# Two attention stages and the feed-forwards behind them: the first two norms of each feed-forward placed among the attention's last slots

## The reference

```python
def _mha(x, y, ..., causal):
    xn, yn = _ln(x, lnx_g, lnx_b), _ln(y, lny_g, lny_b)
    q, k, v = ...                                  # 16 heads of 32
    a = softmax(einsum('bhsd,bhtd->bhst', q, k) * D ** (-0.5))
    if causal: a = a * mask
    o = einsum('bhst,bhtd->bhsd', a, v)
    x_out = x + o @ li1_w + li1_b
    h = gelu(_ln(x_out, ln3_g, ln3_b) @ li2_w + li2_b)
    return x_out + h @ li3_w + li3_b
x = _ln(xx, ln1_g, ln1_b)
x = x + _mha(x, x, a1_..., causal=True)            # self attention, second feed-forward
x = _ln(x, ln2_g, ln2_b)
return x + _mha(x, ee, a2_..., causal=False)       # cross attention, third feed-forward
```

## Time and profile before

| what | before |
|---|---|
| median of 3 runs | 1454.49 us (1454.26 to 1460.39) |
| the profiled execution, its own time | 1445.23 us |
| its span | 1443.5 us |
| TensorE busy | 1334.6 us |
| VectorE busy | 988.5 us |
| ScalarE busy | 845.6 us |
| GpSimd busy | 653.1 us |
| first feed-forward norm behind self attention starts | 965.32 us |
| the same behind cross attention | 1234.29 us |

### The profile page before, as it was taken

How to read it: one execution, slowest core, us unless ns; L and a number is a source line. 1 busy time by engine, 2 the same in 40 slices (tenths; PEclk the granted TensorE clock), 3 DMA queues, 4 the chain that set the end, 5 groups by cost and what they waited for, 6 DMA issues and landing times.

```text
span 1443.5 us, 42854 instructions
## 1 busy us (share of the span) xinstructions
PE 1334.6 (92%) x17894; PEld 872.2 (60%) x17912; DVE 988.5 (68%) x2236; ACT 845.6 (59%) x1325; POOL 653.1 (45%) x1118
## 2 busy tenths in 40 slices
PE   6899999997999999989999999888989999899996
PEld 3455555554455554466677677656767777677685
DVE  5688887875555555578888988645577887676233
ACT  3577777775666566577677677543466666432231
POOL 4455555543001003246666665333347775455255
PEclk7899999998999999999999999999999999999898
DMA  7000000000600000000000000002011111032451
GB/s 222 3 3 3 3 3 3 3 3 2 161 8 0 1 1 1 1 2 32 17 32 21 29 32 21 28 31 60 1 32 46 47 47 46 30 92 85 129 156 52
DMA packets 55186, 53.78 MB, mean 37 GB/s; under 512 B 9305, under 2 KB 49245, under 8 KB 54738
## 3 DMA queue, kind: packets, MB, share of 16 engines
q1 hardware_dynamic: 51154, 44.24, 10.0%
q0 software_dynamic: 2816, 6.11, 1.2%
q10 hardware_dynamic: 1024, 0.69, 0.2%
HBM read 20.34 MB, written 14.49 MB: 24 GB/s over the span
## 4 chain that ended last, share of the span: by engine, by line
PE 64%; DVE 14%; POOL 6%; DMA 5%; issue 4%; SPq 4%; ACT 3%; ACTq 0%; POOLq 0%; DVEq 0%
PE psum L1538 5%; PE psum L941 4%; PE psum L942 4%; PE psum L943 4%; PE psum L1215 4%; PE psum L1566 3%; PE psum L1179 3%; PE psum L2572 3%; PE psum L2547 3%; SPq L795 2%; DVE b_nm L1621 2%; DMA a_QT<-a_nmT 2%; DVE a_nm L603 2%; PE psum L521 2%; DVE c_nm L2069 2%
## 5 line engine op out<-in xcount | busy, mean ns | idle before, releaser
L1621 DVE TENSOR_REDUCE b_nm<-psum 128x4 f16<-128x1024 f32 x128 | 157.2, 1228 | 45.1 <-PE psum L1543 45.0
L720 ACT ACTIVATE a_prob<-psum 128x768 f32<-128x768 f32 (+1 forms) x160 | 136.1, 853 | 63.1 <-PE psum L458 61.4
L603 DVE TENSOR_REDUCE a_nm<-psum 128x4 f16<-128x1024 f32 (+1 forms) x96 | 117.2, 1222 | 42.4 <-PE psum L488 29.0
L772 POOL TENSOR_SCALAR_AFFINE_SELECT a_prob<-a_prob 128x512 f32<-128x512 f32 x128 | 82.1, 641 | 125.5 <-ACT a_prob L720 125.3
L171 POOL TENSOR_TENSOR f_ln_rstd<-f_ln_tmp,pow_half 128x4 f32<-128x4 f32 x24 | 25.4, 1058 | 203.0 <-DVE f_ln_tmp L160 202.9
L1069 ACT ACTIVATE xo_sb<-psum,f_w_h_s 128x512 f32<-128x512 f32 x64 | 44.0, 688 | 85.6 <-PE psum L943 85.6
L1538 PE MATMUL psum<-b_QTh,b_KTh 32*128 32x256 f16 x512 | 70.7, 272 | 16.2 <-DVE b_nm L1621 14.0
L1543 PE MATMUL psum<-b_KTh,b_QTh 32*128 32x256 f16 x512 | 70.8, 274 | 0.0
L1538 PE MATMUL psum<-b_QTh,b_KTl 32*128 32x256 f16 x512 | 69.8, 267 | 0.0
L1538 PE MATMUL psum<-b_QTl,b_KTh 32*128 32x256 f16 x512 | 69.8, 267 | 0.0
L1543 PE MATMUL psum<-b_KTh,b_QTl 32*128 32x256 f16 x512 | 69.6, 269 | 0.0
(11 more groups left out here) (449 smaller groups left out, 4654.5 us busy)
## 6 DMA issues: line engine op xcount, KB each, us to landing
f_h_wh<-b_rden SPq DMA_DIRECT2D x64, 128.0 KB, 2.1
f_h_wh<-c_rden SPq DMA_DIRECT2D x64, 128.0 KB, 2.1
expert_in<-empty SPq DMA_DIRECT2D x8, 662.5 KB, 10.8
m_xt<-expert_in SPq DMA_DIRECT2D x7, 662.5 KB, 5.6
m_w<-in_L_ffn_w_dram SPq DMA_DIRECT2D x16, 256.0 KB
x_sb<-in_x_dram SPq DMA_DIRECT2D x8, 256.0 KB, 4.0
f_w_h_w<-in_L_ffn_h_w_dram SPq DMA_DIRECT2D x2, 1024.0 KB, 7.8
out_dram<-m_send SPq DMA_DIRECT2D x8, 256.0 KB, 2.5
```

The costliest lines, as they stand in the source:

```text
L603: nc.vector.tensor_reduce(out, psum[:, banks, :].rearrange("p i (a b) -> p i a b", a=groups), X, ALU.max, negate=True).then_inc(max_done, 1)
L720: nc.scalar.activation(prob[unit % 5][:, :, 0:width], psum[:, first:first + 2, 0:width], ACT.Exp, scale=SCALE).then_inc(exp_done, 1)
L772: nc.gpsimd.affine_select(out=diagonal, in_=diagonal, compare_op=ALU.is_ge, fill=0.0, base=0, pattern=[[0, 4], [1, P]], channel_multiplier ...
L1621: v.tensor_reduce(self.nm[:, :, :].rearrange("p t (j r) -> p j t r", r=32)[:, 2 * e:2 * e + 2, :, g], self.pr.psum[:, 2:4, :].rearrange("p ...
```

## The change

The constants of both stages get a third bound, `steps`, and GpSimd a bound of its own, `tail_gpsimd`; two tables, `NORMS` and `RSTDS`, name slots behind which parts of norms 0 and 1 are written. `run()` stops VectorE and GpSimd earlier (self attention at slot 122, cross attention at 117 and 119), and `mha_ffn` writes the rest up to `steps` with the norms among them. In self attention the "o" of batch 13 moves from slot 126 to 123 (`SOONER`). In cross attention `tail` falls from 127 to 126, which puts every attention step of the third feed-forward one of its slots later on TensorE, ScalarE and GpSimd.

```diff
     def vector_next(n, slots):
         for slot in slots:
-            if last_slot(n, slot) is not None:
+            if (last_slot(n, slot) or 0) >= before.steps:
                 before.vector_slot(last_slot(n, slot))
...
     def vector_program():
-        for n in range(-2, LAST + 1):
+        for s in range(before.tail_vector, before.steps):
+            before.vector_slot(s)
+            for n, k in before.NORMS.get(s, ()):
+                vector_normed(n, k)
+        for n in range(LAST + 1):
             if n == 0:
-                for s in range(before.tail_vector, before.tail):
-                    before.vector_slot(s)
                 nc.vector.wait_ge(before.av_done, before.values)
...
     def gpsimd_program():
-        for n in range(-2, LAST + 1):
+        for s in range(before.tail_gpsimd, before.steps):
+            before.gpsimd_slot(s)
+            for n in before.RSTDS.get(s, ()):
+                ln.gpsimd_rstd(n)
+        for n in range(LAST + 1):
...
-                if last_slot(n, slot) is not None:
+                if (last_slot(n, slot) or 0) >= before.steps:
                     before.gpsimd_slot(last_slot(n, slot))
...
 # SelfAttention
+    SOONER = 19
-    tail_vector, tail = 8 * B + 1, 8 * B + 2
+    tail, steps, tail_vector, tail_gpsimd = 8 * B + 2, 8 * B + 2, 8 * B - 6, 8 * B - 6
+    NORMS = {8 * B - 6: [(0, 0)], 8 * B - 5: [(0, 1), (1, 0)], 8 * B - 3: [(1, 1)]}
+    RSTDS = {8 * B - 6: [0], 8 * B - 4: [1]}
...
+        if "o" in slots and s == self.U * (B - 3) + self.SOONER:
+            early.append(("o", B - 3))
         return [(part, batch) for part, batch, rest in pairs
-                if rest == 0 and 0 <= batch < B and (batch < B - 2 or part not in self.EARLY)] + early
+                if rest == 0 and 0 <= batch < B and (batch < B - 2 or part not in self.EARLY)
+                and (part, batch) != ("o", B - 3)] + early
...
-        for s in range(self.done + 1, self.tail):
+        for s in range(self.done + 1, self.tail_gpsimd):
             if s == 32:
                 self.pr.clear_old()
             self.gpsimd_slot(s)
...
 # CrossAttention (and the same line in its run())
-    tail_vector, tail = 8 * (B - 1) + 6, 8 * (B - 1) + 7
+    tail, steps, tail_vector, tail_gpsimd = 8 * B - 2, 8 * B - 1, 8 * B - 11, 8 * B - 9
+    NORMS = {8 * B - 11: [(0, 0)], 8 * B - 9: [(0, 1)], 8 * B - 8: [(1, 0)], 8 * B - 4: [(1, 1)]}
+    RSTDS = {8 * B - 9: [0], 8 * B - 7: [1]}
```

## The result

| | before | changed |
|---|---|---|
| median of the runs | 1454.38 us (4 runs, 1450.38 to 1460.39) | 1434.14 us (4 runs, 1432.55 to 1441.22) |
| profiled execution, its span | 1445.23, 1443.5 us | 1433.22, 1431.5 us |

The changed kernel takes 0.9867 of the time before (95% interval 0.9819 to 0.9915). The medians lie 20.2 us apart, the two profiled executions 12.0 us. Three questions follow: did each term come as worked out, what do the medians show that the traces don't, and where do the traces differ in places that the change doesn't touch.

The account below looks back on a forecast made before the run. TensorE, busy 92% of the span, was taken as the bound, so only its gaps could be won: 5.1 + 4.8 + 2.2 = 12.1 us off the 1454.49 us median gave 1442.4 us, range 1437 to 1450.

Parts of the forecast that it names:

- I take the gain off the median: Whole kernel: the 12.1 us gain is subtracted from the runs' median of 1454.49 us, giving 1442.4 us.
- First junction, 5.1 us: Self attention's end into feed-forward: earlier norms bring the last reciprocal and piece 3's transpose 7.3 us sooner, less 2.2 half clock.
- Rival 1: Self attention's end: half clock costs nothing at piece 3's transpose; total gain 14.3 to 15.0 us, chance 0.20.
- rival 2: Self attention's end: weight landing follows traffic, not the reciprocal, so a later wait keeps the time; 1447.5 or 1449.7 us, chance 0.10.
- GpSimd's side: Self attention's end: piece 0's power delays a mask and its value products run 2 us later, hidden with 3 us spare.
- Rival 4: GpSimd's queue, self attention's end: powers waiting for VectorE hold the masks and slow the kernel, 1459.5 us at 20 us lateness; chance 0.04.
- Second junction, 4.8 us: Cross attention's end into feed-forward: earlier norms start the last reciprocal 4.77 us sooner, and piece 2's transpose follows, 4.8 us gained.
- the later slot, 2.2 us: Cross attention's last output product behind piece 0's closing: removes 0.95 us routing-weight wait and about 1.25 us half clock.
- The broadcast: Cross attention's end: the time from batch 14's reciprocal to its scaling on VectorE, held at 5.8 us, the term to question.
- Rival 3: Both junctions: the change doesn't do what it says, as piece 0's transpose may wait on something else; gain 0 to 5, chance 0.06.
- Behind 1276 us: After both junctions TensorE is the bound again, so the time gained stays; a new wait past 1270 us would be wrong.
- 1.79 us alone did nothing: Self attention's end: argument against the free-clock case, that TensorE's clock stayed full behind a single wait of 1.79 us.

Follow-up runs that it names:

- the first comparison: The changed kernel against the kernel before, four runs each, chip not on record: medians 1434.14 and 1454.38 us, ratio 0.9867.
- two larger comparisons: The changed kernel, unedited, measured again against the kernel before: ratios 0.9902 and 0.9904, or 14.2 and 13.9 us less.
- the last comparison: The remaining follow-up kernels and the changed kernel a third time, against the kernel before (median 1452.82 us, 17 runs): changed kernel's ratio 0.9904.
- the old splits: GpSimd splits the next attention's three weights ahead of piece 3's power; the changed kernel with them moved to pieces 2, 3 and 4 measured 0.9870 against before.

## Why the prediction was right or wrong

**The time was wrong, the sum nearly right.** Forecast was a gain of 12.1 us and 1442.4 us; the first comparison gave 1434.14, under the range. The step that failed is "I take the gain off the median", with a range that allowed 2.5 us for the spread of the runs. Against a profiled execution the sum was made, and there it held: 1433.1 forecast, 1433.22 measured. But the medians of four runs each, 20.2 us apart, carry an uncertainty of 7 us; two larger comparisons give 14.2 and 13.9 us. Off 1454.38 that is 1440.3, inside the range. So of the 8.3 us of error, 2 are the size of the gain and some 6 the first comparison's medians. It is the one before that did not come again there: 1454.38, then 1448.55 with 27 runs and 1449.20 with 23, while the changed kernel's 1434.14 was 1434.75 the second time. Both were higher in the last comparison, 1452.82 and 1439.12. Whether the first was chance or the chip, no run shows. The equality of 1433.1 and 1433.22 is luck as well: the changed kernel's first execution gained 5.3 and 8.2 us in the two stretches, 13.5 and not 12.1, it was 2.9 us ahead at the first junction, where nothing had changed, and it lost 3.8 us at its end.

**First junction, 5.1 us: right in mechanism and size.** Six executions have its new order and the old splits, one of them with o(13) in its old slot: five took 86.28 to 88.27 us, the sixth 92.86, their mean is 88.13. Four have the old order, 92.26 to 94.07, mean 92.87. That is 4.7 us, or 5.7 without the sixth. Reciprocal(15) directly behind the last output, z3 by 7.30 us, o(15) with 1.72 us of wait (forecast 1.9), a wait ahead of z3 of 3.4 to 5.05 us (forecast 3.7), half clock behind it: all as stated. Rival 1, the clock costs nothing, fell: all three executions of the change have half clock behind z3, and it cost 1.7 to 2.3 us, where the prediction took 2.2. The 0.7 us that this rival added for a shorter broadcast did come, at the second junction (below). What the prediction lacked is that the term varies: the 22.49 us that it held fixed from reciprocal(15) to z3 took 22.35 to 24.02, with GpSimd going on 4.7 us behind the last issue in one execution and 6.3 in another, and half clock comes or not behind equal waits. This is rival 2 in a weak form.

**GpSimd's side: right.** The value products waited 1.24 us, less than the 1.79 of the earlier trace rows, and never for a mask. That they waited less is not the order's doing: in the other executions it is 1.30 to 2.44 us with the norms moved and 1.79 to 2.31 without, each time for the reciprocal. Rival 4 has nothing for it.

**Second junction, 4.8 us, and the later slot, 2.2 us: together right, wrongly divided.** Forecast 7.0, measured 8.2 against the first execution before and 5.7 against the second; against the mean of the four with the old order there (80.25, 77.77, 79.82, 80.91) it is 79.69 less 72.07, 7.6. The norms without the slot give 3.4 against that mean, the slot on top 4.3. At z2, where 4.8 us were forecast, the change is 5.46 us ahead of the first execution before, counted from the stretch's start, and 3.80 without the slot. The term of the slot was mis-sized: it counted 0.95 us of wait and 1.25 of half clock, which measured 0.89 and 1.70, and put at nothing that o(14) too stands a slot later. With the norms early z0 is ready, and o(14) in front of it then waits 1.57 us for its broadcast, at TensorE's cost; behind the first hidden product it waits for nothing.

**The broadcast.** The sum held it at 5.8 us. From the end of reciprocal(14) to scaled(14) it took 4.97 us (1219.98 to 1224.95), and 4.30 to 5.25 in the nine executions with the norms moved there. It matters little to TensorE, since o(14) no longer waits for it. z2 comes 32.98 to 33.03 us behind the stretch's start in the eight with the new slots, and its norm ends at 32.3 to 33.0; with 5.8 us the norm would end at about 33.5 in the changed kernel's first execution, by an estimate from these rows, and z2 would be some 0.6 us later. That is most of what z2 came sooner than forecast. By the Trainium skill, "DMA: Bandwidth & Descriptors", section "Anatomy of one DMA", the 5.8 us would be 4.2, an estimate from the page's fit; the nine rows all lie between, the lowest 0.1 us above it.

**Rival 3** fell: z0's wait "issue" is gone at both junctions once the norms are early, and is back with 4.15 us in the kernel that has only the new slots.

**Behind 1276 us** the forecast had the shift stay. It did not at the very end. There ScalarE's last activation waits on something that the profile calls remote, and the last products run at half clock. ScalarE is not the first: VectorE's output step ahead of it waits on the same. Both steps read products of TensorE, whose records run without a wait up to 1409.04. The changed kernel's first execution, VectorE, ScalarE and TensorE:

```profile
1411.19 0.29 DVE L2648 TENSOR_TENSOR m_ys<-psum,m_b 128x128 f32<-128x128 f32 x1 [3.62 <-remote]
```

```profile
1412.64 0.80 ACT L2670 ACTIVATE xo_sb<-psum,m_b 128x640 f32<-128x640 f32 x1 [3.50 <-remote]
```

```profile
1413.58 7.61 PE L2589 MATMUL psum<-m_w,xo_sb 128*128 128x128 f32 x40 [4.54 <-ACT xo_sb L2670]
```

The second:

```profile
1414.91 4.70 PE L2589 MATMUL psum<-m_w,xo_sb 128*128 128x128 f32 x40 [0.97 <-ACT xo_sb L2670]
```

It came in 5 of the 14 executions, in old and new orders, in all four of the last comparison and in none of the eight of the two between. It costs 3.8 to 6.2 us of the span: the changed kernel's first execution was 15.8 us ahead of the first before it at the last experts' outputs on VectorE, and its span is 12.0 us shorter; the others are worked out alike, and where the late activation is missing the two shifts agree (10.9 and 10.9 in its second). The comparison in which every profiled execution had it is the one with the median of 1452.82, the two without it had 1448.55 and 1449.20; it ran on another chip than they did, so the chip may be what both hang on. The first profiled execution of the kernel before lacks it, which may be most of the 9.26 us by which it lay under its median; its other runs have no trace, so that stays open, and so does what the two engines wait for.

## What to carry to other kernels

Before a gain is taken off a median, look at what the profiled execution does not share with the other runs. Here runs of the kernel before lay 16 us apart in one comparison, more than the change brought. Traces of one program differed by up to 7.8 us in span (1427.7 and 1435.5); they show half clock that cost 1.7 or 3.4 us in a place, and one late step at the end that cost 3.8 to 6.2. That the same makes the 16 us is not shown, since those runs have no trace. Compare a stretch of the trace between two fixed instructions in several executions; the second junction read 72.05 to 72.17 us in all eight with the new order, where the interval of a ratio left 4.5 us open at best.

When a step is moved ahead because it heads a chain, ask next whether the chain's end needs it: the weights' splits stood in GpSimd's queue ahead of a power that TensorE waited for, and moving them was worth about as much (5.8 us) as the whole move of the norms at that junction (4.7 to 5.7). And a slot that is worth nothing alone can be worth 4.3 us once the step ahead of it is early.

## What was not expected of the hardware

- TensorE's clock after a short wait is not settled by the wait: behind 2.15 us at the same instruction it was 0.50 in one execution and 1.00 in another, behind 0.79 us at the gate product 1.00 in one and 0.50 in another. Nor is it settled by the wait's length: at the value products it fell behind 1.81 us (the change with old output slots) and stayed full behind 2.44 us (with o(13) in its old slot). So the prediction's "1.79 us alone did nothing" could not carry an argument. The two, wait and clock:

```profile
949.35 0.41 PE L1584 MATMUL psum<-f_hT0h,b_group_col 128*32 128x256 f32 x2 [1.81 <-DVE b_rden L1667]
```

```profile
950.00:952.00 2.00, 2.00 (x36) 0.50 0.53 181
```

```profile
956.02 0.41 PE L1580 MATMUL psum<-f_hT0h,b_group_col 128*32 128x256 f32 x2 [2.44 <-DVE b_rden L1663]
```

```profile
956.00:958.00 2.00, 1.98 (x46) 1.00 0.34 114
```

- Summed over the 2 us stretches up to 1424 us, one less the granted clock comes to 27 to 44 us of lost clock in the 14 executions.
- A normalise of four tiles took 1.11 us alone and 2.72 us at 1219.90 with four GpSimd operations of 0.72 to 0.74 us back to back beside it (1219.38 to 1222.54); beside GpSimd's splits 2.28 to 2.30 us. The Trainium skill, "SBUF — State Buffer", section "Who interferes with whom", has VectorE and GpSimd share a pair of ports that one of them holds for a whole instruction, where VectorE runs in a mode that uses both its pairs; the trace agrees in that the normalise ends with the last of the four, but no row shows the mode. Here it cost nothing, since TensorE was at the value products.
- The new order removed not only time but its variation: second stretch 72.05 to 72.17 us in eight executions with it, 77.77 to 80.91 us in four without. In all eight the clock is full over the whole stretch, and TensorE's one wait above 0.3 us is 0.93 us ahead of the first hidden product, so there is little left that the clock or a landing could change.
